# New orders of work on every engine of a software-pipelined block of four layers, and a rearranged setup

## The reference, cut to what matters

```python
x = x + attention(ln(x))      # for each position (a, b): 8 heads over the 16 images, gated by a sigmoid
t = t + moe_top2(ln(t))       # router: softmax over 8 experts, the 2 best, each a 64x64 matrix
x = x + ema_conv(ln(x))       # expand to 128 channels, running mean s = 0.9 s + 0.1 x along a, gate, contract
t = t + soft_moe(ln(t))       # 32 experts, each picks its best 8 of the 4096 tokens of an image
```

## Time and profile before

| | |
|---|---|
| median of 3 runs | 3001.29 us (2978.11 to 3006.42) |
| time of the profiled execution | 2984.94 us |
| its span in the profile | 2983.2 us |
| busy: PE, DVE, POOL, ACT | 86%, 77%, 71%, 55% |
| mean granted clock of TensorE | 0.86 |
| bytes from and to HBM | 55.56 MB read, 50.33 MB written |

### The profile page before, as it was taken

The page is one execution under the profiler, slowest core; times in us unless marked ns, Lnnn a source line. Parts: engine busy times, 40 slices in busy tenths (PEclk is TensorE's granted clock), DMA queues, the critical chain, the costliest instruction groups (busy, mean ns, idle before and its releaser), DMA issues. The chain is left out here.

```text
span 2983.2 us, 127037 instructions
## 1 busy us (share of the span) xinstructions
PE 2574.6 (86%) x45291; PEld 1875.2 (63%) x45291; DVE 2302.6 (77%) x8761; ACT 1639.2 (55%) x3077; POOL 2116.4 (71%) x3094
## 2 busy tenths in 40 slices
PE   2899998888989999998998898889999999998378
PEld 2666666666666666666666666666666666665258
DVE  2677888888887887888888888878888788787536
ACT  2556565656555565656565655656565555554330
POOL 1677777777777777777877777777878777776320
PEclk9888889989898898889888989988888788887579
DMA  0011111111111111110101111111111111110479
GB/s 18 10 19 21 19 18 20 18 20 18 20 19 19 19 18 19 18 20 17 21 17 20 18 19 19 18 20 17 21 17 20 17 20 19 18 19 13 138 242 374
DMA packets 263175, 107.14 MB, mean 36 GB/s; under 512 B 251284, under 2 KB 253882, under 8 KB 259003
## 3 DMA queue, kind: packets, MB, share of 16 engines
q1 hardware_dynamic: 262091, 101.81, 14.6%
q10 hardware_dynamic: 1008, 4.29, 0.4%
HBM read 55.56 MB, written 50.33 MB: 35 GB/s over the span
## 5 line engine op out<-in xcount | busy, mean ns | idle before, releaser
L830 DVE TENSOR_TENSOR yg<-shared,gates 128x512 f32<-128x512 f32 x512 | 347.8, 679 | 188.6 <-PE shared L636 188.1
L506 ACT ACTIVATE kT<-shared,b_k,quarter 128x512 f32<-128x512 f32 x512 | 368.2, 770 | 157.2 <-PE shared L737 157.2
L750 PE MATMUL shared<-w_o,ogT 128*128 128x64 f32 x2048 | 355.2, 347 | 0.0
L439 POOL TENSOR_TENSOR norm_conv<-x,mv_conv 128x256 f32<-128x256 f32 x128 | 78.9, 617 | 378.1 <-DVE mv_conv L929 378.1
L750 PEld LDWEIGHTS shared<-w_o,ogT 128*128 128x128 f32 x2048 | 342.8, 261 | 0.8 <-DVE lg L933 0.3
L522 ACT CAST cT<-shared 128x512 fp32r<-128x512 f32 x128 | 75.1, 587 | 456.4 <-PE shared L660 456.4
L882 DVE TENSOR_REDUCE mixed<-yg 128x256 f32<-128x2048 f32 x128 | 292.6, 2286 | 29.6 <-DVE yg L830 29.4
L635 PE MATMUL shared<-w_expert_hi,tT 128*128 128x512 f32 x512 | 279.5, 546 | 0.0
L378 POOL TENSOR_TENSOR probs<-weights,own_den 128x1024 f32<-128x1024 f32 x128 | 247.6, 1935 | 9.9
L743 PE MATMUL shared<-w_con,gated 128*128 128x64 f32 x1024 | 165.9, 315 | 100.5 <-DVE gated L922 100.5
L634 PE MATMUL shared<-bias,ones 3*128 3x512 bf16 x512 | 215.2, 420 | 38.3 <-ACT lT L518 35.4
(11 more groups left out here) (202 smaller groups left out, 6892.9 us busy)
## 6 DMA issues: line engine op xcount, KB each, us to landing
x_in<-in_x SPq DMA_DIRECT2D x1024, 16.0 KB, 1.7
x_scratch<-x SPq DMA_DIRECT2D x1024, 16.0 KB, 1.5
normalized_x_scratch<-norm_pick SPq DMA_DIRECT2D x1024, 16.0 KB, 1.5
xa<-normalized_x_scratch SPq DMA_DIRECT2D x8, 1024.0 KB, 8.5
xc<-normalized_x_scratch SPq DMA_DIRECT2D x8, 1024.0 KB, 12.4
out_x<-xc SPq DMA_DIRECT2D x16, 512.0 KB, 4.8
xc<-x_scratch SPq DMA_DIRECT2D x4, 1024.0 KB, 9.4
xb<-x_scratch SPq DMA_DIRECT2D x4, 1024.0 KB, 17.2
```

Source lines behind the costliest of these rows:

```text
L506: ins = s.activation(kT[:, h, :], bk("k"), ACT.Identity, bias=b_k[:, h:h + 1], scale=quarter[:, h:h + 1])
L750: ins = t_.matmul(bk("att_out")[:, t * D:(t + 1) * D], ogT[:, h, tile(t)], w_o2[:, h, :], start=(h == 0), stop=(h == 1))
L830: v.tensor_tensor(yg[:, t], bk(y).rearrange("p (d e) -> p d e", e=NE), gates[:, t, :].unsqueeze(1).broadcast_to([P, D, NE]), ALU.mult).the ...
```

## The change

It touches the loop and the setup, and no instruction of either does another computation than before.

- `STAGES`: 24 of the 96 steps get another lag. `pow_att`, `sub_att`, `mul_att`, `lo_att`, `rnd_att` go from 1 to 0; `v`, `scores`, `xbo`, `vA` from 2 to 1; `probs` from 3 to 2; `x1`, `st_ffn`, `ag_ffn`, `sub_ffn` from 4 to 3; `y0`, `y2`, `y3`, `yg1` from 5 to 4; `conv_t`, `cT`, `rnd_conv`, `lo_conv` from 6 to 5; and two go back by one, `gp1` from 2 to 3 and `pick_t` from 8 to 9. `xload`, `st_att` and `ag_att` stay at 0, `x3` and `x3st` at 7, `n3st` at 8.
- `TURNS` and `BANK`: the order on PE and the banks are new. `route`, `att_out` and `scan_out`, of which the latter two followed each other, now have other steps between them.
- POOL, ACT and DVE get new orders. The order on DVE becomes `probsT ag_pick st_att yg3 ag_att yg2 smax yg0 sub mixed og scan lg st_conv max ag_conv gated ssum top2 lgm x1 mrep rec sel st_ffn gden x3 grec st_pick gates ag_ffn yg1`. The order on POOL becomes `r1_ffn pow_ffn mul_ffn r1_pick lo_ffn pow_pick r1_att x2bc pow_att x2 sub_pick sub_att mul_pick sub_conv mul_att r1_conv pow_conv mul_conv xbo own probs lo_conv sub_ffn lo_att`.
- SP keeps its order in a slot: `xload`, `n3st`, `x3st`.
- Setup: ten of SP's weight loads go to ACT's queue, and the two transfers `bias3` and `bv3`, which wait for DVE's setup, as well. Four memsets (`gated`, `qT`) go from DVE to POOL, and DVE does those parts of its setup first that don't wait for ACT.

The PE, POOL and ACT blocks are moved as wholes, and only DVE's is quoted, where the prediction needs it.

```diff
@@ -33,24 +33,25 @@
 
 
 STAGES = {
-    0: "xload r1_att st_att ag_att",
-    1: "pow_att sub_att mul_att lo_att rnd_att zT qA km0 km1 att_t q k",
-    2: "xbo own vA exp gateA gp1 scores v gate smax sub ssum rec",
-    3: "probs values att_out probsT og",
-    4: "sub_ffn r1_ffn pow_ffn mul_ffn lo_ffn rnd_ffn tT lge ffn_t y1 route x1 st_ffn ag_ffn lg max top2 "
-       "lgm mrep sel gden grec gates",
-    5: "x2 sub_conv r1_conv pow_conv mul_conv y2 y0 y3 yg1 yg2 yg0 yg3 mixed st_conv ag_conv",
-    6: "lo_conv x2bc rnd_conv cT exA ema conv_t expand scan",
+    0: "xload r1_att pow_att sub_att mul_att lo_att rnd_att st_att ag_att",
+    1: "xbo zT vA km0 qA km1 att_t v k q scores",
+    2: "own probs exp gateA gate smax sub ssum rec",
+    3: "sub_ffn gp1 values att_out probsT og x1 st_ffn ag_ffn",
+    4: "r1_ffn pow_ffn mul_ffn lo_ffn rnd_ffn tT lge ffn_t route y1 y3 y2 y0 lg max top2 lgm mrep sel "
+       "gden grec gates yg1",
+    5: "x2 sub_conv r1_conv pow_conv mul_conv lo_conv rnd_conv cT conv_t yg3 yg2 yg0 mixed st_conv "
+       "ag_conv",
+    6: "x2bc exA ema expand scan",
     7: "x3st scan_out gated x3 st_pick",
-    8: "n3st r1_pick sub_pick pow_pick mul_pick pick_t ag_pick",
-    9: "lT picks pick",
+    8: "n3st r1_pick pow_pick sub_pick mul_pick ag_pick",
+    9: "lT picks pick_t pick",
 }
 LAG = {name: lag for lag, names in STAGES.items() for name in names.split()}
-TURNS = ["scores", "y2", "y0", "conv_t", "y3", "expand", "v", "att_t", "values", "gate", "ffn_t", "pick", "q", "y1",
-         "route", "k", "scan_out", "att_out", "pick_t"]
-BANK = {"scores": (4, 5), "y2": (0,), "y0": (2,), "conv_t": (1,), "y3": (3,), "expand": (2,), "v": (0,), "att_t": (1,),
-         "values": (4, 5, 6, 7), "gate": (0,), "ffn_t": (1,), "pick": (3,), "q": (2,), "y1": (1,), "route": (3,),
-         "k": (2,), "scan_out": (0,), "att_out": (3,), "pick_t": (0,)}
+TURNS = ["pick_t", "att_t", "expand", "ffn_t", "values", "route", "gate", "v", "k", "att_out", "q", "pick", "scan_out",
+         "y1", "y3", "scores", "y2", "conv_t", "y0"]
+BANK = {"pick_t": (0,), "att_t": (2,), "expand": (1,), "ffn_t": (0,), "values": (4, 5, 6, 7), "route": (0,),
+         "gate": (3,), "v": (2,), "k": (3,), "att_out": (0,), "q": (2,), "pick": (1,), "scan_out": (0,), "y1": (2,),
+         "y3": (1,), "scores": (4, 5), "y2": (2,), "conv_t": (0,), "y0": (3,)}
 PEELED = 6
 
 
@@ -203,7 +204,7 @@
             s_n3_store = [sem(f"n3_stored{q}") for q in range(2)]
 
             N_LOADS = 34
-            N_POOL_SETUP = 11
+            N_POOL_SETUP = 15
             N_DVE_SETUP = 16
 
             def at(i, q, name, back=0):
@@ -266,6 +267,16 @@
             block = cols.enter_context(nc.Block())
 
 
+            def rows_loads(k):
+                rows = slice(k * D, (k + 1) * D)
+                be = b_exp.rearrange("(h d) -> h d", h=2).unsqueeze(2)
+                return [(lnw_col[rows], ln_w.unsqueeze(1)), (lnb_col[rows], ln_b.unsqueeze(1)),
+                        (w_raw[rows, 0, :], Wq), (w_raw[rows, 1, :], Wk), (w_raw[rows, 2, :], Wg), (w_raw[rows, 3, :], Wv),
+                        (w_router[rows], router_w), (w_expert[rows], expert_w.rearrange("e d c -> d e c")),
+                        (bprim_col[rows], be[0]), (bgate_col[rows], be[1])]
+
+            lower_loads = rows_loads(1)
+
             @block.sync
             def _(sp):
                 loads = [(bg_col[:], bg.unsqueeze(1)), (w_o[:], Wo),
@@ -274,21 +285,11 @@
                          (rb_rows[:], router_b.unsqueeze(0).broadcast_to([P, NE])),
                          (gw_raw[:], gate_w),
                          (bias_row[:], expert_b.rearrange("e c -> (e c)").unsqueeze(0))]
-                be = b_exp.rearrange("(h d) -> h d", h=2).unsqueeze(2)
-                for k in range(2):
-                    rows = slice(k * D, (k + 1) * D)
-                    loads += [(lnw_col[rows], ln_w.unsqueeze(1)), (lnb_col[rows], ln_b.unsqueeze(1)),
-                              (w_raw[rows, 0, :], Wq), (w_raw[rows, 1, :], Wk), (w_raw[rows, 2, :], Wg), (w_raw[rows, 3, :], Wv),
-                              (w_router[rows], router_w), (w_expert[rows], expert_w.rearrange("e d c -> d e c")),
-                              (bprim_col[rows], be[0]), (bgate_col[rows], be[1])]
+                loads += rows_loads(0)
                 loads += [(gb_col[k * EP:(k + 1) * EP], gate_b.unsqueeze(1)) for k in range(4)]
                 for dst, src in loads:
                     sp.dma_start(dst, src).then_inc(s_weights, 16)
-                assert len(loads) + 3 == N_LOADS, len(loads)
-
-                sp.wait_ge(s_dve_setup, N_DVE_SETUP)
-                sp.dma_start(bias3[:], bias_parts[:]).then_inc(s_bias3, 16)
-                sp.dma_start(bv3[:], bv_parts[:].rearrange("o k t c -> o k (t c)")).then_inc(s_bias3, 16)
+                assert len(loads) + 3 + len(lower_loads) == N_LOADS, len(loads)
 
                 def step(i, q):
                     if runs(i, q, "xload"):
...
                 setup(g.memset(minus_half[:], -0.5))
+                for q in range(2):
+                    setup(g.memset(qT[q][:], 0.0))
+                    setup(g.memset(gated[q][:], 0.0))
                 setup(g.memset(ones3[:], 1.0), True)
                 assert n_setup[0] == N_POOL_SETUP, n_setup[0]
                 pool.wait_ge(s_weights, 16 * N_LOADS)
                 pool.wait_ge(s_dve_setup, N_DVE_SETUP)
...
                 act.dma_start(wcon_raw[:], W_con.unsqueeze(1).broadcast_to([D, 2, D])).then_inc(s_weights, 16)
+                for dst, src in lower_loads:
+                    act.dma_start(dst, src).then_inc(s_weights, 16)
                 act.wait_ge(s_weights, 16 * N_LOADS)
...
                 act.wait_ge(s_act_setup, 10)
                 act.wait_ge(s_dve_setup, N_DVE_SETUP)
+                act.dma_start(bias3[:], bias_parts[:]).then_inc(s_bias3, 16)
+                act.dma_start(bv3[:], bv_parts[:].rearrange("o k t c -> o k (t c)")).then_inc(s_bias3, 16)
+                act.wait_ge(s_pool_setup, N_POOL_SETUP)
 
...
                 dve.wait_ge(s_weights, 16 * N_LOADS)
-                dve.wait_ge(s_act_setup, 10)
-                v.memset(gated[0][:], 0.0)
-                v.memset(gated[1][:], 0.0)
-                v.memset(qT[0][:], 0.0)
-                v.memset(qT[1][:], 0.0)
-                v.tensor_copy(w_qkg_hi[:], w_scaled[:, 0:3, :])
-                v.tensor_copy(w_expert_hi[:].rearrange("d (c e) -> d c e", e=NE), w_expert[:].rearrange("d e c -> d c e"))
-                v.tensor_copy(bias_parts[:, 0, :].rearrange("o (c e) -> o c e", e=NE),
-                              bias_row[:].rearrange("o (e c) -> o c e", e=NE))
+                by_channel = lambda a: a.rearrange("d (c e) -> d c e", e=NE)
+                by_expert = w_expert[:].rearrange("d e c -> d c e")
+                every_tile = lambda a: a.unsqueeze(1).broadcast_to([1, QT, HC])
+                v.tensor_copy(by_channel(w_expert_hi[:]), by_expert)
+                v.tensor_copy(by_channel(bias_parts[:, 0, :]), bias_row[:].rearrange("o (e c) -> o c e", e=NE))
                 setup(v.tensor_reduce(odd_even[:], block_of[:].rearrange("p (x j) -> p j x", j=2), AX.X, ALU.add))
-                setup_join()
-                setup(v.tensor_tensor(w_qkg_lo[:], w_scaled[:, 0:3, :], w_qkg_hi[:].bitcast(F32), ALU.subtract))
...
+                    if runs(i, q, "ag_pick"):
+                        z = par(q, "ag_pick")
+                        wait_apart(dve, (s_bn["pick"], at(i, q, "ag_pick")), (s_norm["pick"], at(i, q, "ag_pick", 2)))
+                        for t in range(QT):
+                            ins = v.bn_aggr(mv["pick"][z][:, t, :], bn["pick"][z][:, t, :])
+                        ins.then_inc(s_agg["pick"], 1)
+                    if runs(i, q, "st_att"):
+                        z = par(q, "st_att")
+                        dve.wait_ge(s_x[z], stored(i, q, "st_att"))
+                        for t in range(QT):
+                            ins = v.bn_stats(bn["att"][z][:, t, :], x_in[z][:, t, :])
+                        ins.then_inc(s_bn["att"], 1)
+                    if runs(i, q, "yg3"):
+                        gated_expert(3)
+                    if runs(i, q, "ag_att"):
+                        z = par(q, "ag_att")
+                        wait_apart(dve, (s_bn["att"], at(i, q, "ag_att")), (s_norm["att"], at(i, q, "ag_att", 2)))
+                        for t in range(QT):
+                            ins = v.bn_aggr(mv["att"][z][:, t, :], bn["att"][z][:, t, :])
+                        ins.then_inc(s_agg["att"], 1)
...
-                    if runs(i, q, "st_att"):
-                        z = par(q, "st_att")
-                        dve.wait_ge(s_x[z], stored(i, q, "st_att"))
-                        for t in range(QT):
-                            ins = v.bn_stats(bn["att"][z][:, t, :], x_in[z][:, t, :])
...
+                    if runs(i, q, "gden"):
```

(57 more changed lines are left out.)

552 lines of the change are left out of this document (249 added, 303 removed).

## The result

The changed kernel takes 3489.23 us (median of 4 runs, 3485.33 to 3495.66) against 2998.82 us before (4 runs, 2978.11 to 3006.42): a ratio of 1.166, 95% interval 1.162 to 1.170. Its profiled execution took 3486.61 us, with a span of 3484.9 us. The predicted 3420 us is 2% low, and the range of 3240 to 3540 holds the time.

The account below looks back on a forecast made before the run. Before, no engine was full; orders and waits set the pace at 20.98 us a slot. Forecast: 120 slots at 24.9 (+470), five at 17.9 (-15), setup -20, on 2984.94: 3420 us, range 3240 to 3540.

Parts of the forecast that it names:

- The chain through SP: Loop: DVE from `st_att` to `x3`, 13.9 us, plus SP from `x3` to the next loaded data, 9.9: 23.8 a slot.
- The clock: PE resumes at the lower clock after idling before `att_t`, delaying later steps: 1.1 us a slot, bounds 0 and 2.1.
- the second rival: The SP chain binds, but PE's lower clock costs nothing on it: 23.8 us a slot, 3288 us; chance 0.30.
- The rival without clock cost: Same as the second rival: DVE's work covers PE's delay or the clock holds, 3288 us; chance 0.30.
- The rival of 17.9 us a slot: Loop: the design works and DVE's work sets the slot, 17.9 us, 2574 us in all; chance 0.06.
- Setup and the end of the loop: Setup saves 20 us; the five slots from last load to last `mixed` run at 17.9 us, 15 less.
- DVE's wait for `x_in`: Sign in the loop: DVE idle before `st_att` for 6 to 8 us in each slot, ended by the transfer.
- PE's idle time: Sign in the loop: PE idle for some 5 us before `att_t`, with a granted clock of 0.50 after it.
- `x1` waiting for PE: Sign on DVE: `x1` waits for PE in slots without `scan`; no size given.
- the first `st_att`: Sign of the setup: DVE's first `st_att` starts near 22 us.
- SP's wait for `x3`: Sign on SP: no long wait except for `x3`, in place of that for `mul_pick`.
- `sub_conv`: Sign on POOL: this step has hardly a wait, where before it waited 2.98 us a slot.

Follow-up runs that it names:

- e3: The changed kernel with 20 unused matmuls more on PE in each slot, in front of `pick_t`: 3315.97 us, ratio to before 1.104.
- e2: The changed kernel with both stores one slot later (`n3st` lag 9, `x3st` lag 8): 2737.72 us, ratio to before 0.911.
- e5: The kernel before with both stores one slot later (`n3st` lag 9, `x3st` lag 8) and nothing else: 2987.66 us, ratio to before 0.999.
- e7: e2 with `xbo` in front of `mul_conv` on POOL, `st_att` two DVE steps later and `ag_att` with it: 2638.61 us, ratio to before 0.881.
- e4: The kernel before with the changed setup alone: 2982.57 us, ratio to before 0.994.
- e10: The changed kernel with the setup of the kernel before: 3511.81 us, ratio to before 1.171.
- e1: The changed kernel with the store `x3st` alone one slot later (lag 8 in place of 7): 3131.64 us, ratio to before 1.042.
- e9: e8 with 20 unused matmuls more on PE in each slot, in front of `ffn_t`: 3193.32 us, ratio to before 1.064.
- e8: The changed kernel with `st_att` two DVE steps later and `ag_att` with it, stores left in place: 3517.71 us, ratio to before 1.174.

## Why the prediction was right, and where it was off

**The chain through SP: right, cause and size.** Predicted were 9.9 us over SP and 13.9 on DVE without the clock, 23.8 in all. Measured are 9.68 in the changed kernel, and 13.73 where the clock is held up (e3), 23.4 in all. e2 shows that this chain is what costs the time, and e5 that the same edit does nothing where the load is covered. The rule of the Trainium skill ("DMA: Bandwidth & Descriptors", Rules for kernel authors), to issue a transfer early and wait for it late, held here: in e2 only the issue is moved ahead, and the slot falls from 25.07 to 19.15 us.

**The clock: right in kind, the term too small.** I took 1.1 us, the middle of 0 to 2.1. e3 gives 1.9 as the mean (15.66 - 13.73). In most slots the half level ended during `values` or just behind it (4.1 us after PE resumed, by the median), and the median stretch of 15.00 us is what I had forecast; but in 20 of 94 slots of the trace it lasted 12 us (15 slots) or 23 us (5 slots), through `route`, `gate`, `v` and `k`, and there the stretch is 18.2 to 20.5 us. One of them is this, whose `x1` waited 3.58 us:

```profile
1169.67 1.11 PE L657 MATMUL shared<-ident,split_att 128*128 128x128 f32 x4 [5.94 <-DVE yg L834]
...
1174.32 1.87 PE L689 MATMUL shared<-w_router,tT 128*128 128x8 f32 x8
...
1177.71 2.08 PE L703 MATMUL shared<-w_scaled,zT 128*128 128x128 f32 x8
...
1183.01 0.42 DVE L942 TENSOR_TENSOR x<-shared,x_bo 128x256 f32<-128x256 f32 x1 [3.58 <-PE shared L717]
```

My bound of 2.1 us counted `att_t` to `gate` only. This is nearly the whole miss: in the steady slots the clock's term was 0.8 us too small and the other two together 0.4 too large. From the 7th to the 122nd interval of `mixed` the slot is 25.45 us against the 24.9 of the forecast, and 0.55 us in 120 slots are 66 us, where the profiled execution lies 67 above 3420. That every burst starts at the lower level after such a wait, as the Trainium skill has it ("TensorE: Matmul & The Clock Gate", HAM oscillation), agrees with the trace: `att_t` takes 1.11 or 1.12 us in 91 of 94 slots, and 0.99 to 1.05 in the others. That rule excludes only one way to the second rival, that the clock holds, and not the other, that DVE covers PE's delay.

**The rival without clock cost, 3288 us (0.30).** Ruled out: DVE does not cover PE's delay. With the cost taken away (e3) the time is 3316 us, within 1% of that rival's figure, so its price was right and its condition was not met.

**The rival of 17.9 us a slot, 2574 us (0.06).** It is near what the orders can do without the chain: e2, which moves only the stores, comes to 19.15 us and 2738 us, and e7, which moves three steps more, to 18.32 us and 2639 us. The change as made could not, since the 16 issues stand in the way, as the prediction said.

**Setup and the end of the loop: right.** 20 us predicted; the first `mixed` comes 20.9 us (e4) and 20.2 us (against e10) earlier. The parts are right too: ACT's wait for the weights ends at 14.15 us in place of 20.43, 4.3 us of DVE's setup stand behind ACT's last copy, and the wait for x is gone. The last five intervals sum to 88.3 us (18.26, 17.68, 18.76, 15.34, 18.25), 17.7 each, as the 17.9 that I took.

**What should be seen after.** Right: DVE's wait for `x_in` in every slot (5.9 us, just under the 6 to 8 I gave), PE's idle time of 5 to 6 us before `att_t` with 0.50 behind it, `x1` waiting for PE in about every second slot, the first `st_att` at 22 us. Wrong in two places. I wrote that SP's wait for `x3` would come in place of that for `mul_pick`; it came beside it (9.9 and 2.8 us a slot). The wait for `mul_pick` is slack, since `n3st` is through before `x3` comes, and it turned into the bound as soon as the wait for `x3` was taken away (e1). And `sub_conv` was to have hardly a wait, but has 1.5 us a slot; with the same order on POOL it has 0.3 in e2 (6.0 us in 400), and in e3, whose slot is long but whose clock is held up, 0.2:

```profile
POOL norm_conv L424 <- DVE mv_conv L915: 3.5, 10, 1.3
```

So in this order on DVE that wait goes with the lower clock and not with the long slot.

## What to carry to other kernels

For each step that a new order brings forward, write down what it waits for, and follow that back through the queue that issues it to the steps for which this queue waits first; the slot is at least as long as this loop, whatever the engines' busy shares say. When a queue issues in order, put the transfers that nobody awaits soon behind a wait that is a slot old. And when TensorE must stand still for 5 to 6 us, as here, what resumes behind the wait runs at half the clock for some microseconds. Unused work in the wait itself took that away (e3, e9); to put work there that nobody waits for is the other way, which no run tried.

## What the runs showed of the hardware

Adding work made a kernel faster: e9 has 4.8 us more of matmuls in each slot than e8 and takes 9% less time. And the lower level did not last equally long. After PE's waits of 5 to 6 us in the changed kernel it lasted 2.7 to 5.2 us in three slots of four and 12 or 23 us in a fifth of them, with the same steps behind it; in e8, where `values` and `route` resume in place of `att_t` and `expand`, it lasted 7.5 to 9.6 us. Why a fifth of the slots differ, and what in those steps makes e8's longer, was not tried.
